# A fused attention and feed-forward kernel: the second feed-forward round goes from step 23 to step 21, an output-projection unit from step 21 to step 24, and the up weights go ahead of the gate weights

## The reference, cut to what matters

```python
# x: (4, 1024, 256) float32; 16 heads of 64; hidden size 768
q, k, v = x @ Wq, x @ Wk, x @ Wv                     # per head
attn = softmax(causal(q @ k.T / sqrt(64)))
y = layernorm(x + concat_heads(attn @ v) @ Wo, eps=1e-3) * gamma + beta
x = layernorm(x + y)
gate, up = x @ (w_gate / 127).T, x @ (w_up / 127).T
x = layernorm(x + (silu(gate) * up) @ (w_down / 127).T)
```

## Time and profile before

| | |
|---|---|
| median of 3 executions | 1459.61 us (1457.96 to 1460.11) |
| the profiled execution's own time | 1458.47 us |
| its span, first to last instruction | 1456.7 us |
| granted TensorE clock, mean | 0.989 of full speed |
| TensorE matmul busy | 1405.5 us, 96% of the span |
| VectorE busy | 1030.1 us, 71% |
| ScalarE busy | 1001.9 us, 69% |
| GpSimd busy | 985.7 us, 68% |
| chain that ended last | PE 74%, ACT 11%, DVE 8%, POOL 4% |

### The profile page before, as it was taken

One profiled execution on the slowest core, in us unless ns is written; L12 is line 12 of the kernel. 1 busy time (PEld: TensorE's weight loads), 2 busy tenths in 40 slices (PEclk: granted clock), 3 DMA queues, 4 the chain that ended last, 5 costly groups with the idle time before them and its releaser, 6 DMA issues.

```text
span 1456.7 us, 23745 instructions
## 1 busy us (share of the span) xinstructions
PE 1405.5 (96%) x7936; PEld 1228.6 (84%) x7936; DVE 1030.1 (71%) x2747; ACT 1001.9 (69%) x1924; POOL 985.7 (68%) x926
## 2 busy tenths in 40 slices
PE   6999999999999999999999999999999999999977
PEld 5788888888888888888888888888888888888866
DVE  7777776767776766777667676776767677677874
ACT  4777777867676676867668676676767668676534
POOL 4665666556676775867768586775867768588744
PEclk9999999999999999999999999999999999999988
DMA  4323222313342132312233122132313223121000
GB/s 132 100 81 101 54 66 95 117 52 93 103 119 73 52 96 59 110 53 59 74 117 95 52 60 73 56 120 59 96 39 116 74 60 95 52 62 56 23 12 29
DMA packets 61240, 110.44 MB, mean 76 GB/s; under 512 B 16256, under 2 KB 41600, under 8 KB 61120
## 3 DMA queue, kind: packets, MB, share of 16 engines
q1 hardware_dynamic: 61120, 108.94, 25.0%
HBM read 60.95 MB, written 13.89 MB: 51 GB/s over the span
## 4 chain that ended last, share of the span: by engine, by line
PE 74%; ACT 11%; DVE 8%; POOL 4%; issue 3%; DMA 1%; ACTq 0%; SPq 0%; POOLq 0%
PE bank L797 23%; PE bank L770 15%; PE bank L670 8%; PE bank L746 8%; PE bank L733 7%; PE bank L695 5%; PE bank L832 5%; PE bank L844 3%; ACT probs_hi L982 2%; ACT probs L979 2%; POOL probs_lo L1423 2%; ACT y_tail L1018 1%; ACT Q L962 1%; ACT K L962 1%; POOL h_lo L1465 1%
## 5 line engine op out<-in xcount | busy, mean ns | idle before, releaser
L1423 POOL TENSOR_TENSOR probs_lo<-probs,probs_hi 128x512 fp32r<-128x512 f32 x576 | 747.4, 1305 | 417.4 <-ACT probs_hi L982 413.9
L979 ACT ACTIVATE probs<-bank 128x512 f32<-128x512 f32 x576 | 344.2, 598 | 302.3 <-DVE bank L1180 216.8
L770 PE MATMUL bank<-Q,K 128*128 128x512 f32 (+3 forms) x1536 | 386.3, 353 | 4.2 <-ACT probs_hi L982 4.1
L982 ACT ACTIVATE probs_hi<-bank 128x512 fp32r<-128x512 f32 x576 | 342.2, 594 | 0.0
L770 PEld LDWEIGHTS bank<-Q,K 128*128 128x128 f32 x1536 | 252.2, 190 | 34.7 <-ACT probs_hi L982 7.5
L746 PE MATMUL bank<-K,Q 128*128 128x512 f32 (+3 forms) x768 | 245.5, 362 | 2.7 <-DVE K L1131 2.1
L1164 DVE CUSTOM_DVE_ANT_0 bank<-bank,mask_keys_free 128x128 f32<-128x128 f32 (+3 forms) x512 | 242.9, 505 | 3.5 <-PE bank L746 3.0
L797 PE MATMUL bank<-probs_hi,VH 128*128 128x512 f32 (+3 forms) x768 | 232.7, 343 | 7.9 <-POOL probs_lo L1423 7.2
L797 PE MATMUL bank<-probs_lo,VH 128*128 128x512 f32 (+3 forms) x768 | 234.6, 346 | 0.0
L797 PE MATMUL bank<-probs_hi,VL 128*128 128x512 f32 (+3 forms) x768 | 234.5, 346 | 0.0
L1180 DVE TENSOR_TENSOR bank<-bank,mask_queries_free 128x256 f32<-128x256 f32 (+1 forms) x320 | 119.3, 373 | 130.6 <-PE bank L770 130.1
(11 more groups left out here) (171 smaller groups left out, 2220.0 us busy)
## 6 DMA issues: line engine op xcount, KB each, us to landing
Q<-Q SPq DMA_DIRECT2D x64, 256.0 KB, 3.7
K<-K SPq DMA_DIRECT2D x64, 256.0 KB, 3.6
recip_bc<-recip_scratch SPq DMA_DIRECT2D x62, 256.0 KB, 3.4
wh<-w_scratch SPq DMA_DIRECT2D x12, 768.0 KB, 4.3
wl<-w_scratch SPq DMA_DIRECT2D x12, 768.0 KB, 5.9
wo_quad<-wo SPq DMA_DIRECT2D x16, 256.0 KB, 3.2
y<-x SPq DMA_DIRECT2D x16, 256.0 KB, 3.8
x_tail<-x SPq DMA_DIRECT2D x13, 256.0 KB, 3.0
```

The costliest lines, as they stand in the source:

```text
L770: last = mm(bk[:, at:at + cols], KX[:, n, P * i:P * i + P], QX[:, n, q0:q0 + cols], start=(KX is K1 and at == 0), stop=(KX is K2 and at + ...
L979: A(pe_[:, g % 2, :], stb[g % 2][:, :], ACT.Exp).then_inc(exp_done, 1)
L982: A(ph[:, g % RING, :], stb[g % 2][:, :], ACT.Exp).then_inc(hi_done, 1)
L1423: G.tensor_tensor(pl[:, g % RING, :], pe_[:, g % 2, :], ph[:, g % RING, :].bitcast(F32), ALU.subtract).then_inc(lo_done, 1)
```

## The change

Three things are edited. The output projection's last unit goes from step 21 to step 24 (`WO_AT`), in iterations 1 to 14, and in iterations 5 to 14 waits there for the second round's `t_glu_up` (`h1`), whose bank 1 it takes. The second round's `t_up` goes from step 23 to step 21 (`STEADY`), and with it its tanh, `t_glu` and `t_glu_up` from 24 to 22 and its `t_hl` from 25 to 23; its `down` stays in step 26. In every round the eight matmuls by the up weights now come ahead of the eight by the gate weights; in the second round the up weights wait for P0's unit 2 and the gate weights for P0's unit 3, which was issued in step 20. The numbered list `PEC` and the tanh's wait follow that order.

```diff
--- before.py
+++ after.py
@@ -150,7 +150,7 @@
 
 
 P1_AT, P1_AT_FIRST = [-1, 0, 1, 2], [-5, -4, -3, -2]
-WO_AT, WO_AT_LAST = [12, 14, 15, 21], [11, 13, 15, 16]
+WO_AT, WO_AT_LAST = [12, 14, 15, 24], [11, 13, 15, 16]
 P0_AT = [17, 18, 19, 20]
 V_AT, V_AT_FIRST = [32, 34, NST + 4, NST + 6], [24, 26, 28, 30]
 LOAD_RAW_AT, RAW_HI_AT, RAW_LO_AT = [3, 4, 9, 10], [7, 8, 10, 12], [8, 9, 11, 13]
@@ -168,7 +168,7 @@
                 DOWN=down, Y2=[a + 1 for a in down], LN3=down[2] + 1, LN3R=down[2] + 2, OUT=down[2] + 3, STORE=store)
 
 
-STEADY = tail_at(-5, -1, 7, [9, 23, 29], [13, 26, 32], 36)
+STEADY = tail_at(-5, -1, 7, [9, 21, 29], [13, 26, 32], 36)
 LAST_A = dict(tail_at(-5, -1, 7, [9, 18, 22], [12, 21, 25], 30), LN3=27, LN3R=28, OUT=29)
 LAST_B = tail_at(8, 11, 19, [21, 25, 29], [24, 28, 32], 36)
 
@@ -314,7 +314,7 @@
         PL = numbered(["xb", "e1", "r1", "m1", "s1", "gam", "add", "e2", "r2", "m2", "s2", "hl0", "hl1", "hl2",
                        "e3", "r3", "m3", "s3"])
         AC = numbered(["n1a", "n1b", "n2a", "n2b", "x1hi", "tanh0", "tanh1", "tanh2", "n3a", "n3b"])
-        PEC = numbered(["tr", "g0", "u0", "d0", "g1", "u1", "d1", "g2", "u2", "d2"])
+        PEC = numbered(["tr", "u0", "g0", "d0", "u1", "g1", "d1", "u2", "g2", "d2"])
         ND, NP, NA, NPE = len(DV), len(PL), len(AC), len(PEC)
 
         FDV = numbered(["xb", "st1a", "st1b", "mv1a", "mv1b", "c1a", "c1b", "a1a", "a1b", "st2a", "st2b", "mv2a", "mv2b", "x1lo"]
@@ -720,6 +720,8 @@
                         pe.wait_ge(v_lo, 4 * it + 4)
                 elif it == NIT - 1:
                     pe.wait_ge(y_added, 4 * wi + 2)
+                elif running(it):
+                    pe.wait_ge(tdve[0], ND * (it - TAIL_LAG) + DV["h1"])
                 else:
                     pe.wait_ge(proj_lo, 2 * proj_unit(it + 1, 0, 2) + 2)
                 if u == 0:
@@ -820,10 +822,13 @@
                 else:
                     pe.wait_ge(tdve[g], ND * n + DV[f"y2{r - 1}"])
                     if g == 0 and r == 1:
-                        pe.wait_ge(y_added, 4 * it)
                         if it + 1 < NIT:
-                            pe.wait_ge(proj_lo, 2 * proj_unit(it + 1, 0, 3) + 2)
-                for W, bk in ((Wg, T[g].bk[0]), (Wu, T[g].bk[1])):
+                            pe.wait_ge(proj_lo, 2 * proj_unit(it + 1, 0, 2) + 2)
+                        else:
+                            pe.wait_ge(y_added, 4 * it)
+                for W, bk in ((Wu, T[g].bk[1]), (Wg, T[g].bk[0])):
+                    if W is Wg and g == 0 and r == 1 and it + 1 < NIT:
+                        pe.wait_ge(proj_lo, 2 * proj_unit(it + 1, 0, 3) + 2)
                     for q in range(2):
                         m = 2 * r + q
                         cnt = 0
@@ -1046,7 +1051,7 @@
                 A(T[g].x1h, two(T[g].bk[1][:, :]), ACT.Copy).then_inc(tact[g], 1)
 
             def t_tanh(n, r, g):
-                act.wait_ge(tpe[g], NPE * n + PEC[f"u{r}"])
+                act.wait_ge(tpe[g], NPE * n + PEC[f"g{r}"])
                 if r:
                     act.wait_ge(tpool[g], NP * n + PL[f"hl{r - 1}"])
                 A(T[g].th, two(T[g].bk[0][:, :]), ACT.Tanh, scale=0.5 * WSCALE).then_inc(tact[g], 1)
```

## The result

The changed kernel takes 1488.2 us (median of 4 runs, 1487.1 to 1489.2) against 1458.8 for the kernel before (4 runs on the same chip, 1456.0 to 1460.1): a ratio of 1.0207, 95% interval 1.0195 to 1.0219, so 2.1% slower. Of the loss of 42 us that I worked out, 12.6 did not come.

What follows compares the result with a forecast made beforehand. TensorE was taken as the bound. Ten iterations of -0.49 + 0.87 + 1.5 + 1.55 = 3.43 give 34.3 us, with 7.8 for iterations 1 to 4 it is 42, forecasting 1501 us, range 1482 to 1512.

Steps and rivals of the forecast that it cites:

- -0.49, the wait in step 26: Step 26, steady iterations: the down product's wait for GpSimd's `h_lo` goes, 0.49 us less per iteration.
- 0 for the swap: All tail rounds: up weights ahead of gate weights cost nothing, since the tanh waited for all sixteen matmuls before and still does.
- 0 for the moves: Steps 21 to 25: matmuls and unit leave one step and enter another, net 0 us on TensorE.
- +0.87, the gate in step 21: Step 21, steady iterations: gate weights wait for VectorE's remainders of P0's unit 3, 0.87 us lost per iteration.
- +1.5, `max_bank` in step 24: Step 24, steady iterations: `max_bank` waits for VectorE's read of step 23's maximum, 1.5 us lost per iteration.
- +1.55, the row ahead of step 27: Step 27, steady iterations: scores wait for the maxima's row, issued by in-order SyncE behind `load_wo` after X; 1.55 us lost each.
- X: Time the moved unit ends, 0.35 us after step 25 starts; `load_wo` may go out only then.
- +7.8 for iterations 1 to 4: Iterations 1 to 4, no tail: step 27's wait for the row costs 2.36 + 1.6 + 1.6 + 2.3 us, 7.8 in all.
- A: Step 27: the row arrives in time, so the third wait and the 7.8 fall away; 1478 us, 7 in 100.
- B: Step 24: VectorE reaches step 23's maximum sooner, or bank order does not bind; without the 1.5, 1486 us; 8 in 100.
- C: Faster: the wait in step 26 goes and no new one comes; -4.9, 1455 us; 2 in 100.
- D: Worse: the row needs 5.9 us instead of 5.2 in 14 iterations; +10, 1511 us; 13 in 100.

Runs made afterwards that it cites:

- the late load: Changed kernel with SyncE's `load_wo` moved from step 23 to step 25, behind the row of maxima: 1474.5 us; same edit in the kernel before: 1458.1 us.
- the gate's split: Changed kernel with second-round tanh and VectorE work in step 23, remainder in 24, up weights in step 21, gate weights in 22: 1472.7 us, ratio 1.0100.
- the kernel with the order alone: Kernel before with only SyncE's order changed: row of maxima first, then reciprocals, then output weights: 1457.0 us, ratio 0.9989.
- reciprocals first: Changed kernel with `load_wo` behind the reciprocals' load in step 24, the row of maxima still last: 1475.7 us, ratio 1.0117.
- the arithmetic one step later: Changed kernel with the second round's tanh and VectorE arithmetic in step 23 instead of 22, its remainder in 24: 1483.9 us, ratio 1.0180.

## Why the prediction was right in sign and its loss 13 us too high

**-0.49, the wait in step 26: right.** With nothing else in the way, step 26 is 0.49 shorter (the late load in the changed kernel).

**0 for the swap: right.** Ratio 1.0006.

**0 for the moves: right in the steady iterations, not in iterations 1 to 4.** There, step 21 is 1.54 shorter and steps 23 and 24 together 1.95 longer. The extra 0.4 is a wait that I had not looked for: with the unit gone from step 21, TensorE reaches the products with V of step 23 before GpSimd has made `probs_lo` (in iteration 2 it waits, at 240.13, for a GpSimd operation that runs until 240.07). The unit had covered that. In the steady iterations sixteen matmuls of the tail stand in its place and cover it too. Over steps 21 to 25 the moves cost 0.24 an iteration. In the steady ones step 22 is 0.18 shorter, a little more than the 0.14 that I had taken for the scores behind the unit, and step 25 as much longer.

**+0.87, the gate in step 21: right.** Measured 0.86 in iteration 10, and 0.85 as the gate's split took it away.

**+1.5, `max_bank` in step 24: right in mechanism, 0.2 too high.** Measured 1.28. The read was put at 918.95 - 914.08 = 4.87 after the start of step 22; in the trace that step starts at 932.80 and the read ends at 937.54, 4.74 after it, while TensorE comes to step 24 in 3.01 instead of 3.05. The restart, for which I had added 0.1, costs nothing here: the matmul behind `max_bank` starts 0.34 after it, but it started 0.32 after it before the change too, with no wait. So a part of the restart was counted that was already in the row.

**+1.55, the row ahead of step 27: this is the step that was mis-sized.** Measured 0.46 + 0.07 = 0.53 on average, 0.57 + 0.08 in iteration 10. It accounts for 10.2 of the 13.7 us by which the steady iterations were put too high; `max_bank` accounts for 2.2 and step 29, below, for 1.3. X was right (0.35 after step 25's start, measured 0.38 to the issue behind it), and so was the distance from X to step 27 without a wait (3.73). The failing number is "5.2 from `load_wo` to step 27", with 4.7 as its lower end: it is 4.30 in iteration 10, 4.19 in iterations 1 and 2 and 4.00 to 4.34 in all but iteration 4, each time with a real wait. SyncE and the scores that waited, iterations 2 and 4 of after:

```profile
244.37 0.39 SPq L482 DMA_DIRECT2D wo_quad<-wo  x1
...
245.37 0.70 SPq L456 DMA_DIRECT2D Q<-neg_max  x1
...
248.56 0.70 PE L772 MATMUL bank<-Q,K 128*128 128x512 f32 x2 [1.25 <-ACT probs_hi L987]
...
403.70 0.39 SPq L482 DMA_DIRECT2D wo_quad<-wo  x1
404.14 0.47 SPq L424 DMA_DIRECT2D raw<-w_down_T  x1
...
405.23 0.71 SPq L456 DMA_DIRECT2D Q<-neg_max  x1
...
409.44 0.89 PE L772 MATMUL bank<-Q,K 128*128 128x512 f32 x2 [2.80 <-issue]
```

In iteration 2 the bracket names ScalarE's `probs_hi`, but its last one had ended at 247.92, 0.64 before the scores start, and what step 27 needs is the one before that. The landing of the row in the trace's records is at 248.47, and in each of the 14 iterations the scores start 0.09 to 0.10 behind it.

The row leaves 1.0 us after `load_wo`. In the earlier trace rows it left 241.31 - 239.62 = 1.69 after it, and I took that as the time that three issues need. It was not. SyncE's rows in that place of before:

```profile
239.11 0.46 SPq L468 DMA_DIRECT2D recip_scratch<-recip  x1
239.62 0.59 SPq L482 DMA_DIRECT2D wo_quad<-wo  x1
240.81 0.46 SPq L476 DMA_DIRECT2D recip_bc<-recip_scratch  x1
```

The reciprocals go out 1.19 after `load_wo`, but only 1.70 after their own store was issued at 239.11, and they wait for that store to land: `recip_stored` stands at their row in the order list ahead of the prediction. In the changed kernel that store has landed before X (in iteration 10 at 938.38, X is 940.51; with the late load, the reciprocals go out at 926.14, 1.9 ahead of `load_wo`), so that wait is not in the distance, and the three leave back to back. I carried over a distance between two instructions that contained a wait for a third, which does not move with them. Of the 0.69 between 1.69 and 1.0, the wait is about 0.5, and the rest is the first issue, 0.39 instead of 0.59.

The other 0.2 of the 0.9 lies behind the row's issue. In iteration 1 of before the records have the row landed 2.98 after its issue, 0.4 before the scores could use it, so its bound of 5.16 was in truth 4.76. In iteration 2 the row took 3.68, where with the same two loads ahead of it it takes 2.93 to 3.25 in the changed kernel. What made iteration 2 slow is open; it shows again (3.65) in the kernel with the order alone.

Transfers ahead of it do delay the row, as the ring-order rule of the Trainium skill (DMA: Bandwidth & Descriptors, Queues, rings and completion order) has it: by the trace's records of transfers it lands 3.20 after its issue in iteration 10, 2.4 where only the output weights' load is close ahead and 1.80 with none.

The page's fixed cost of some 2.0 us whatever the size (Anatomy of one DMA) is given there for the DMAs of GpSimd's path, while the row is issued by SyncE. By it the row would have been in time. The 1.80 that it takes alone is near that figure, but in the changed kernel it took 2.93 to 4.12, so the figure does not serve where loads stand ahead.

**+7.8 for iterations 1 to 4: 7.6 measured, but out of errors that cancel.** The four lost 1.45, 1.37, 0.72 and 4.05, where I had 2.36, 1.6, 1.6 and 2.3. The row costs 0.9 to 1.0 less than I put in iterations 1 to 3 (4.19 to 4.34 instead of 5.2) and 0.2 less in 4 (5.74 instead of 5.9); the moves cost 0.24 more in each. That iteration 4 lost 4.05 has a reason of its own, told below, and makes up for the others by luck.

**Not foreseen: 0.13 given back in step 29** in each steady iteration. It comes with the wait ahead of step 27 and goes with it in the two experiments that end that wait.

**The rivals.** A (the row in time, 1478) is what those two experiments make of the kernel: 1474.5 and 1475.7. The point that I had named for it, scores of step 27 within 4 us of X, was missed by 0.33 us in iteration 10 and by 0.04 in iteration 12. Had I read the wait in SyncE's list and taken 0.5 to 0.7 off the 5.2, the sum would have been 27 to 29 for the steady iterations and 5 to 6 for the early ones, some 1492 to 1495. The last 4 to 7 us could not be had from the rows that I showed. B (step 24's wait away) and C did not hold at any place. D (5.9 everywhere) came near in iteration 4 alone, 5.74.

## What to carry to other kernels

Before a distance between two rows is carried over to a new place, look at each instruction between them for what it waits for: a wait that is over in the new place is no part of the distance. When a unit of work is moved on the bound engine, follow its completion event as well, above all into an in-order DMA list, where a load that nobody needs soon can hold up a small transfer that is needed at once; put the small one first. And a gap that the moved unit covered for another engine (`probs_lo` here) opens where it was taken from.

## What was not expected of the hardware

**A wait can cost twice, through the clock.** Iteration 4 of after, stretches before, in and behind the wait of 2.80 (columns as above; the last but two is the granted clock):

```profile
402.00:406.70 4.70, 4.64 (x27) 3.89 (x25) 2.73 (x10) 2.09 (x6) 2.53 (x3) 1.00 0.34 116
406.70:409.40 2.70, 0.00 (x0) 0.00 (x0) 0.15 (x2) 0.55 (x2) 2.27 (x3) 1.00 0.84 265
409.44:413.10 3.66, 3.66 (x9) 2.86 (x10) 1.06 (x3) 1.20 (x3) 1.18 (x1) 0.55 0.94 312
413.10:417.00 3.90, 3.90 (x22) 3.46 (x21) 2.37 (x5) 3.30 (x7) 2.52 (x4) 0.99 0.43 131
```

TensorE stood still for 2.8 us, and the 3.7 us behind that ran at a granted clock of 0.55, about the lower of its two levels (1.2 of 2.4 GHz), with 512-column matmuls 0.43 apart instead of 0.23. Steps 27 and 28 were longer by 0.95 and 0.65: 1.6 of the 4.05 that this iteration lost.

The same shows in iteration 4 of two other kernels, and costs 1.6 us in steps 27 and 28 in each. With the split gate it comes behind an idle time of 1.94 (0.61 over 3.1 us). With the arithmetic one step later it comes behind 2.54:

```profile
408.68:411.88 3.20, 3.20 (x9) 2.57 (x10) 1.04 (x3) 1.08 (x2) 0.99 (x2) 0.62 0.94 306
```

It does not show in the kernel that moves only the unit, behind 2.50 (1.00). The idle times of up to 1.7 us ahead of step 27 in iterations 1 to 3 left the clock at 1.00 in all of these kernels, and so did the shorter ones of the steady iterations. What decides between 1.94 with a loss and 2.50 without is open; no run was made for it.

**A small transfer's landing depends on what stands ahead of it in its queue, and on how close.** The row of 4 KB, from its issue to its landing in the records:

| ahead of it | us | where |
|---|---|---|
| nothing issued in the last 1.4 us | 1.80 to 1.93 | before, iterations 5 to 14 |
| output weights, issued 0.43 earlier | 2.14 to 2.49 | reciprocals first, iterations 5 to 14 |
| reciprocals, issued 0.51 earlier | 2.58 to 2.85 | late load, iterations 7 to 14 |
| both, 1.0 and 0.51 earlier | 2.93 to 3.25 | after, all but iterations 0 and 4 |
| both and a third load | 4.12 | after, iteration 4 |

The second and third line have one load of 256 KB each, and the fourth has two. So counting loads is not enough: that of the reciprocals directly ahead costs most of the delay, and the output weights ahead of it some 0.4 more. Why the two loads of the same size differ, no run shows.

**The same issue has different lengths.** `load_wo` took 0.39 us of SyncE when it had been waiting idle. In before it was always issued 0.5 behind the store of the reciprocals, and took 0.59 in iterations 1 to 4 but 0.84 to 1.31 in iterations 5 to 14. What makes that difference no run shows.

**A wait taken away comes back in part.** Without the waits ahead of step 27 in iterations 2 to 4, step 28 is 0.26 to 0.31 longer with the row first (0 to 0.29 with the late load), because the products with V wait; a third of the 2.4 us that were won there stays unrealised.
